# The cosine pass of a fused graph network: eight blocks pruned from the product, a moved wait, and a new order on ScalarE

## The chip, the cores and the metric

One Trainium2 chip, one core. The metric is the device time of one execution in microseconds; the kernel before takes 1676.99 us (median of 3 runs, 1675.86 to 1677.04).

## The reference, cut to what matters

Four layers on a graph of N = 3327 nodes with 64 features; `adj` is a dense 3327x3327 float32 matrix with few entries that are not zero. The first three layers are not touched. The fourth runs this twice (it = 0, 1), and only the lines from `cos` to `connectivity` are computed by the changed stage:

```python
att = softmax(Q @ edge_feat.T * scale * H, axis=1); att_scores = att.mean(axis=0)
comp_mask = softmax(0.5*structural + 0.5*att_scores) >= th_comp
x_comp = x * comp_mask[:, None];  xn = x_comp / max(norm(x_comp), 1e-8)
cos = xn @ xn.T
edge_scores = softmax(cos * H, axis=1)
edge_mask = (edge_scores >= th_edge) & comp_mask[:, None]
H_pruned = H * edge_mask
connectivity = H_pruned.sum(axis=1)            # and H_pruned.sum(axis=0)
agg = (H_pruned.T * dv_isqrt) @ transformed * de_inv
x = relu(dv_isqrt * (H_pruned @ agg) @ Theta)
```

## The kernel before, in words

The matrix is padded to 26 row blocks (NB) of 128 rows by 3328 columns, 1.7 MB each, and is streamed from HBM again in every pass. Each of the two iterations runs five passes over the 26 blocks: edge, att, cos, down, up. Rows lie as two halves of 1664 columns (HALF). Engines wait for each other by hand-written counting semaphores; each engine's program is one fixed order.

The **cosine pass** for block k, engine by engine:

- TensorE makes `cos` in four pieces of 2x416 columns in PSUM (`piece`), and for block k-2 sums the columns of the pruned rows (`columns`, which then raises `block_done`).
- VectorE (`cosine_pass`): four times `product_piece` (L1543: PSUM times the adjacency rows in the slot, into the product buffer `prod[k % 2]`, with the row maximum), then `product_max` (L1554, `negmax`), then `prune(k-1)`. Piece 0 of block k waits until the product buffer is free: for `product_free` (ScalarE's sign of block k-2) and for `share_marked` (GpSimd's marks of block k-2).
- ScalarE, the loop that calls `exps`, `sum_share` and `sign`: the exponential of block k over the product (L1247, with the row sum), then the sum of GpSimd's share of block k-1 (L1272), then `sign(k)` (L1263), which writes one mask byte for every column into the arena; the bytes are what `down` and `up` prune with later (L1730, L1759), and here `prune` too.
- GpSimd (`cut_of`, `prune_share`), for the first 24 blocks (SHARED): when the exponential of block k is done it makes the row's threshold `cut` (L637), then the marks of the last 288 columns of each half (SHARE, L647) and multiplies these columns of the slot by them (L650).
- `prune(k)` on VectorE: for k < 24 the first 1376 columns of each half (OWN), slot times (mask byte <= 0), after `sign(k)` (L1694). The last two blocks have no GpSimd share; VectorE makes their `cut` (L1681) and prunes all 3327 columns by comparing the product with `cut` (L1699).

In ScalarE's loop and in VectorE's pass the order is:

```python
for k in range(NB):                      # ScalarE
    exps(f"cos{it}", k)
    if 0 < k <= SHARED:
        sum_share(k - 1)
    sign(k)
```

The cosine pass keeps its blocks in four slots. SyncE issues the load of block k+4 into the slot of block k when `columns(k)` and `sum_share(k)` are both done (L538 and the wait behind it in `late_stream`). The last four blocks stay for the down pass; the first three loads of the down pass go into memory that the cosine pass frees at its very end, the rest into slots that are free once the down pass has used them. Behind the cosine pass stand the row sums, a softmax over nodes, and the down pass.

Below, E(k) is the start of the exponential of block k on ScalarE.

Of the kernel before, what the change touches and what calls it, by code (L numbers as in the profile page):

```python
# [24 lines left out]
ALU = mybir.AluOpType  # L25
# [8 lines left out]
NB = (N + P - 1) // P  # L34
# [77 lines left out]
def place(row):  # L112

    return 2 * (row % HB) + row // HB
# [40 lines left out]
SHARE = 288  # L155
OWN = HALF - SHARE
SHARED = NB - 2
PRUNES = NB + NB - KEPT_BLOCKS


# [47 lines left out]
def build_program(nc, adj, adj_t, x_nodes, early_weights, late_weights, rows, bq, consts, decay_consts, x_kept, out):  # L208
    ctx = ExitStack()
    with ctx:  # L210
        def sb(name, cols, dt):
            return ctx.enter_context(nc.sbuf_tensor(name, [P, cols], dt))

        def sem(name):
            return ctx.enter_context(nc.semaphore(name))
# [9 lines left out]
        prod = [pairs[:, i * NP:(i + 1) * NP] for i in range(2)]  # L225
# [63 lines left out]
        cut = sb("cut", 2, F32)  # L289
# [29 lines left out]
        def halves(t):  # L319

            return t.rearrange("p (h n) -> p h n", h=2)
# [90 lines left out]
        row_cut = sem("row_cut")  # L412
        pruned = sem("pruned")
        share_marked = sem("share_marked")
# [76 lines left out]
        def _(sp):  # L491
# [36 lines left out]
            def late_stream(name, source, first=0, last=NB):  # L528
                kind, it = name[:-1], int(name[-1])
                for k, row in enumerate(ROW_ORDER[kind]):  # L530
# [4 lines left out]
                    behind = free - 1 - BASE[f"cos{it}"]  # L535
                    if kind in ("cos", "down") and 0 <= behind < SHARED:

                        sp.wait_ge(share_summed, it * SHARED + behind + 1)  # L538
                    if name == "edge1" and home > 5 and k < 8:
# [8 lines left out]
                    if kind == "down" and home == 8 and k < 7:  # L548

                        sp.wait_ge(piece_read, (2 * it + 2) * NB * 4 + 5)  # L550
                        sp.wait_ge(pruned, it * PRUNES + NB - 1)
                        sp.wait_ge(product_free, (2 * it + 2) * NB + 1)
                    if kind == "down" and home == 5 and k < 7:

                        sp.wait_ge(pruned, it * PRUNES + NB)
                        sp.wait_ge(product_free, (2 * it + 2) * NB + 2)
# [50 lines left out]
        def _(pool):  # L607
# [22 lines left out]
            def cut_of(it, k):  # L630

                pool.wait_ge(piece_read, ((2 * it + 1) * NB + k) * 4 + 4 + 5)
                pool.memset(prod[k % 2][:, N:NP], -HUGE)
                pool.wait_ge(exp_done, (2 * it + 1) * NB + k + 1)
                one = slice(k % 2, k % 2 + 1)
                at = place(ROW_ORDER["cos"][k])
                pool.tensor_scalar(cut[:, one], rowsum[:, one], thresholds(it)[1], small["blocked"][:, at:at + 1],  # L637
                                   ALU.mult, ALU.add).then_inc(row_cut, 1)

            def prune_share(it, k):  # L640
# [3 lines left out]
                pool.wait_ge(row_cut, it * NB + k + 1)  # L644
                if it * SHARED + k:
                    pool.wait_ge(share_pruned, it * SHARED + k)
                pool.tensor_scalar(marks, product, cut[:, k % 2:k % 2 + 1], None, ALU.is_ge)\  # L647
                    .then_inc(share_marked, 1)
                pool.wait_ge(share_marked, it * SHARED + k + 1)
                pool.tensor_tensor(slot, slot, marks, ALU.mult).then_inc(share_pruned, 1)  # L650
# [8 lines left out]
            for it in range(2):  # L659
# [8 lines left out]
                pool.tensor_scalar(tiny["unused_step"][:, :], ones32[:, 0:1], 1.0, None, ALU.mult).then_inc(steps_ready, 1)  # L668
                for k in range(SHARED):
                    cut_of(it, k)  # L670
# [7 lines left out]
        def _(pe):  # L678
# [222 lines left out]
            def product(name, left, right):  # L901
# [19 lines left out]
                def columns(k):  # L921
# [4 lines left out]
                    else:  # L926
                        pe.wait_ge(pruned, it * PRUNES + k + 1)
                        if k < SHARED:
# [62 lines left out]
            for it in range(2):  # L991
# [69 lines left out]
                def turn(pair, it=it):  # L1061

                    for g, rows_ in enumerate((range(16), range(16, NB))):
                        if pair:
                            pe.wait_ge(turned_sbuf, it * NB + 2 * (pair - 1) + g + 1)
                        for q in rows_:
                            last = pe.transpose(ps[:, 4 * BANK + q * D:4 * BANK + (q + 1) * D].bitcast(BF16),  # L1067
                                                sign_pairs[:, q * HALF + pair * P:q * HALF + (pair + 1) * P],
                                                ident_b[:, :])
                        last.then_inc(turned_psum, 1)  # L1070

                pe.wait_ge(down_ready, 2 * it + 1)
                for k in range(NB):
                    if k == NB - 1:
                        pe.wait_ge(edeg_read, it + 1)
                        turn(0)
                    pe.wait_ge(pruned, it * PRUNES + NB + max(0, k - KEPT_BLOCKS + 1))
                    if k == KEPT_BLOCKS:
# [36 lines left out]
        def _(act):  # L1115
# [104 lines left out]
            for it in range(2):  # L1220
# [22 lines left out]
                def exps(name, k):  # L1243
                    bufs = products_of(name)
                    act.wait_ge(negmax_ready, PRODUCTS.index(name) * NB + k + 1)
                    b = k % len(bufs)
                    act.activation(bufs[b][:, 0:N], bufs[b][:, 0:N], ACT.Exp, bias=negmax[:, b:b + 1],  # L1247
                                   accum_out=rowsum[:, b:b + 1]).then_inc(exp_done, 1)
# [11 lines left out]
                def sign(k):  # L1260
                    act.wait_ge(row_cut, it * NB + k + 1)
                    row = ROW_ORDER["cos"][k]
                    act.activation(interleaved(sign_marks[:, row * NP:(row + 1) * NP]), halves(prod[k % 2][:, 0:NP]),  # L1263
                                   ACT.Sign, bias=cut[:, k % 2:k % 2 + 1], scale=-1.0, saturate=False)                        .then_inc(product_free, 1)
# [9 lines left out]

                for k in range(NB):
                    exps(f"cos{it}", k)
                    if 0 < k <= SHARED:
                        sum_share(k - 1)
                    sign(k)
                root(small["structural"][:, :], small["edeg"][:, :], deg_sq, it + 1, deg_rt)  # L1280
                node_exp(2 * it + 1)
                act.wait_ge(colsum_psum, 2 * it + 2)
# [55 lines left out]
        def _(dve):  # L1338
# [190 lines left out]
            def product_piece(name, k, c):  # L1529
                g, bufs = PRODUCTS.index(name), products_of(name)  # L1530
                if c == 0:
                    landed(dve, name, k)
                    if name.startswith("cos"):

                        dve.wait_ge(product_free, g * NB + k + 1)
                        if k >= 2:
                            dve.wait_ge(share_marked, g // 2 * SHARED + min(k - 1, SHARED))
                    elif k >= 3:

                        dve.wait_ge(product_free, g * NB + k - 2 + 2)  # L1540
                        dve.wait_ge(tail_weighted, g // 2 * ADDED + min(k - 2, ADDED))
                dve.wait_ge(piece_ready, (g * NB + k) * 4 + c + 1)
                dve.tensor_tensor_reduce(out=pieces3(bufs[k % len(bufs)], c),  # L1543
                                         in0=pieces_psum(piece_place(name, k, c)[0]),
                                         in1=pieces3(slot_of(name, k), c), scale=1.0, scalar=-3.0e38, op0=ALU.mult,
                                         op1=ALU.max, accum_out=max4[:, 4 * (k % 2) + c:4 * (k % 2) + c + 1])\
                    .then_inc(piece_read, 1)
# [63 lines left out]
            for it in range(2):  # L1611
# [3 lines left out]
                for c in range(0 if it else 1, 3):  # L1615
# [21 lines left out]
                                              op1=ALU.mult))  # L1637
# [4 lines left out]
                def weigh(k):  # L1642
# [8 lines left out]
                                              in1=S["imp"][:, 2 * TAIL:NB], op0=ALU.mult, op1=ALU.add))  # L1651
# [33 lines left out]
                def prune(k):  # L1685
                    slot = slot_of(f"cos{it}", k)
                    row = ROW_ORDER["cos"][k]
                    conn = S["conn"][:, place(row):place(row) + 1]
                    if k < SHARED:

                        dve.wait_ge(product_free, (2 * it + 1) * NB + k + 3)
                        own = halves(slot[:, :])[:, :, 0:OWN]
                        marks = interleaved(signs[:, row * NP:(row + 1) * NP])[:, :, 0:OWN]
                        dve.scalar_tensor_tensor(out=own, in0=marks, scalar=0.0, in1=own, op0=ALU.is_le, op1=ALU.mult,  # L1694
                                                 accum_out=conn).then_inc(pruned, 1)
                    else:

                        dve.wait_ge(row_cut, it * NB + k + 1)
                        dve.scalar_tensor_tensor(out=slot[:, 0:N], in0=prod[k % 2][:, 0:N],  # L1699
                                                 scalar=cut[:, k % 2:k % 2 + 1], in1=slot[:, 0:N], op0=ALU.is_ge,  # L1700
                                                 op1=ALU.mult, accum_out=conn).then_inc(pruned, 1)
                cosine_pass(f"cos{it}", cut_of, prune)


                dve.wait_ge(pruned, it * PRUNES + NB)
                dve.wait_ge(share_summed, (it + 1) * SHARED)
# [5 lines left out]
                def degrees():  # L1712
# [9 lines left out]
                                              op0=ALU.is_ge, op1=ALU.mult))  # L1722
# [48 lines left out]
                for k in range(2, NB):  # L1771
                    up(k)
                    if it == 1 and k == NB // 2:
# [3 lines left out]
                                                 op0=ALU.mult, op1=ALU.mult)  # L1777
# [116 lines left out]
```

## Time and profile before

| | |
|---|---|
| median of 3 runs | 1676.99 us |
| the profiled execution: time, span | 1675.23 us, 1673.4 us |
| TensorE busy | 1476.8 us, 88% of the span |
| VectorE busy | 1140.3 us, 68% |
| ScalarE busy | 729.7 us, 44% |
| GpSimd busy | 349.3 us, 21% |
| HBM, mean over the span | 345 GB/s |
| cosine pass, iteration 0 | from 664.5 us to 849.3 us of the span |
| cosine pass, iteration 1 | from 1273.5 us to 1458.6 us |

Busy shares are means over stages that have different limits. What a stage is worth is read in that stage: by the idle time in front of each instruction and what ended it.

### The profile page before, as it was taken

The numbers are of one execution on the slowest core, as the hardware profiler recorded it, in microseconds if no ns is written. First come the engines' busy times: TensorE is split into PE (matmuls) and PEld (weight loads), VectorE is DVE, ScalarE is ACT, GpSimd is POOL, SyncE is SP. The second block draws the span as 40 slices with busy tenths as digits, with TensorE's granted clock in tenths as the row PEclk, the third lists the DMA queues.
The fourth block names the chain that finished last, engine by engine and source line by source line (L and its number), as shares of the span: only waits on it lengthen the run. The fifth ranks groups of instructions, "written<-read, shape, count | busy, mean of one in ns | idle before, by whom it ended". The sixth has DMA issues, their size and how long they took to land.

```text
span 1673.4 us, 24337 instructions
## 1 busy us (share of the span) xinstructions
PE 1476.8 (88%) x10187; PEld 634.7 (38%) x10187; DVE 1140.3 (68%) x1615; ACT 729.7 (44%) x665; POOL 349.3 (21%) x305
## 2 busy tenths in 40 slices
PE   6789999999999999677888799999997887798896
PEld 2234434434344344333332344443343333332443
DVE  0000213677611998999989799206997999999897
ACT  0000101533211675999940243023776999900443
POOL 0000000000000795444400000002993444200000
PEclk9999999999999999999899999999999889999999
DMA  9979598799799997466689999999993767699995
GB/s 401 427 314 409 213 426 341 253 317 411 298 424 386 426 425 307 168 246 245 241 326 427 424 413 423 427 426 423 420 410 147 253 246 258 232 405 426 426 425 208
DMA packets 62620, 578.41 MB, mean 346 GB/s; under 512 B 6320, under 2 KB 6576, under 8 KB 23472
## 3 DMA queue, kind: packets, MB, share of 16 engines
q1 hardware_dynamic: 62512, 576.87, 85.3%
q8 instruction: 80, 1.31, 0.3%
q14 instruction: 28, 0.23, 0.0%
HBM read 575.14 MB, written 1.70 MB: 345 GB/s over the span
## 4 chain that ended last, share of the span: by engine, by line
PE 56%; DMA 18%; DVE 16%; issue 7%; ACT 2%; SPq 0%; POOL 0%; DVEq 0%; POOLq 0%; ACTq 0%
PE ps L685 54%; DMA arena<-adj_t 9%; DMA slot<-adj 5%; DVE slot L1730 4%; DVE shared L1543 4%; DVE slot L1759 2%; DMA shared<-adj_t 2%; DVE shared L1730 2%; DMA slot<-adj_t 2%; DMA arena<-adj 1%; PE ps L1067 1%; DVE shared L1759 1%; ACT shared L1294 1%; ACT shared L1247 1%; DVE slot L1699 0%
## 5 line engine op out<-in xcount | busy, mean ns | idle before, releaser
L685 PE MATMUL ps<-shared 64*128 64x416 f32 (+3 forms) x1292 | 280.0, 474 | 89.1 <-DVE max L1543 86.3
L1543 DVE CUSTOM_DVE_ANT_1 shared<-ps,slot 128x832 f32<-128x832 f32 x352 | 342.0, 1021 | 5.7 <-PE ps L685 5.1
L1247 ACT ACTIVATE shared<-shared,negmax 128x3327 f32<-128x3327 f32 x88 | 270.1, 3069 | 68.1 <-DVE negmax L1554 65.5
L685 PE MATMUL ps<-slot,cur 128*64 128x512 f32 (+1 forms) x1440 | 262.9, 515 | 17.0 <-DVE slot L1730 14.8
L622 POOL TENSOR_SCALAR cur<-shared,row_rz 128x768 f32<-128x768 f32 x32 | 70.5, 2204 | 866.7 <-DVE row_rz L1645 862.1
L685 PE MATMUL ps<-arena 64*128 64x416 f32 (+1 forms) x1072 | 208.4, 525 | 1.5 <-DVE max L1543 0.9
L1294 ACT ACTIVATE shared<-ps 128x2048 int16<-128x2048 int16 (+1 forms) x52 | 78.1, 1554 | 276.1 <-PE ps L1067 276.0
L685 PEld LDWEIGHTS ps<-shared 64*128 64x128 f32 (+2 forms) x1292 | 113.6, 162 | 222.3 <-DVE max L1543 130.8
L685 PEld LDWEIGHTS ps<-slot,cur 128*64 128x64 f32 x1440 | 96.6, 137 | 179.7 <-issue 154.5
L1263 ACT ACTIVATE arena<-shared,cut 128x3328 fp8e4<-128x3328 f32 x52 | 159.0, 3059 | 2.1 <-DVE cut L1681 1.2
L1694 DVE SCALAR_TENSOR_TENSOR slot<-arena,slot 128x2752 f32<-128x2752 int8 x48 | 145.0, 3021 | 5.4 <-ACT arena L1263 5.4
L685 PE MATMUL ps<-shared,cur 128*64 128x512 f32 (+1 forms) x672 | 125.9, 522 | 15.5 <-DVE shared L1730 7.7
L1351 DVE COPY shared<-ps 128x512 f32<-128x512 f32 x3 | 2.1, 692 | 191.6 <-PE ps L685 191.6
L685 PEld LDWEIGHTS ps<-arena 64*128 64x128 f32 (+1 forms) x1072 | 87.3, 175 | 109.6 <-issue 69.1
L1759 DVE SCALAR_TENSOR_TENSOR slot<-shared,slot 128x3328 f32<-128x3328 int8 x32 | 114.5, 3621 | 10.7 <-ACT shared L1294 8.5
L685 PE MATMUL ps<-slot,ones 128*32 128x128 f32 (+3 forms) x1456 | 106.3, 422 | 6.7 <-DVE slot L1699 6.7
L685 PE MATMUL ps<-shared,arena 128*64 128x320 bf16 (+4 forms) x798 | 105.4, 360 | 0.4 <-DMA shared<-adj 0.4
L685 PE MATMUL ps<-slot,arena 128*64 128x512 f32 x496 | 90.8, 515 | 4.1 <-DMA slot<-adj 4.1
L1189 ACT ACTIVATE shared<-ps 128x512 int16<-128x512 f32 x104 | 53.7, 517 | 88.9 <-PE ps L685 88.6
L1123 ACT ACTIVATE shared<-ps 128x640 f32<-128x640 f32 (+1 forms) x6 | 3.9, 650 | 196.9 <-PE ps L685 196.9
L1730 DVE SCALAR_TENSOR_TENSOR slot<-arena,slot 128x3328 f32<-128x3328 int8 x24 | 85.9, 3622 | 2.9 <-DMA slot<-adj 2.9
L647 POOL TENSOR_SCALAR share_marks<-shared,cut 128x576 bf16<-128x576 f32 x48 | 82.4, 1717 | 4.7
(203 smaller groups left out, 1596.6 us busy)
## 6 DMA issues: line engine op xcount, KB each, us to landing
slot<-adj SPq DMA_DIRECT2D x157, 1664.0 KB, 9.8
slot<-adj_t SPq DMA_DIRECT2D x60, 1664.0 KB, 14.1
arena<-adj_t SPq DMA_DIRECT2D x52, 832.0 KB, 6.6
shared<-adj SPq DMA_DIRECT2D x26, 1664.0 KB, 13.9
arena<-adj_t SPq DMA_DIRECT2D x25, 1664.0 KB, 22.9
shared<-adj_t SPq DMA_DIRECT2D x22, 1664.0 KB, 14.8
arena<-adj SPq DMA_DIRECT2D x15, 1664.0 KB, 14.9
slot<-adj SPq DMA_DIRECT2D x2, 1024.0 KB, 18.8
```

What stands on the lines that cost most here:

```text
L622: weighted = pool.tensor_scalar(halves(dst), product, row_rz[:, k % 3:k % 3 + 1], None, ALU.mult)
L647: pool.tensor_scalar(marks, product, cut[:, k % 2:k % 2 + 1], None, ALU.is_ge)\
L685: return pe.matmul(o, l, r, start=start, stop=stop, skip_group_check=True)
L1067: last = pe.transpose(ps[:, 4 * BANK + q * D:4 * BANK + (q + 1) * D].bitcast(BF16), sign_pairs[:, q * HALF + pair * P:q * HALF + (pair + 1 ...
L1189: act.activation(dst, bank(c, w), ACT.Relu).then_inc(relu_act, 1)
L1247: act.activation(bufs[b][:, 0:N], bufs[b][:, 0:N], ACT.Exp, bias=negmax[:, b:b + 1], accum_out=rowsum[:, b:b + 1]).then_inc(exp_done, 1)
L1263: act.activation(interleaved(sign_marks[:, row * NP:(row + 1) * NP]), halves(prod[k % 2][:, 0:NP]), ACT.Sign, bias=cut[:, k % 2:k % 2 + 1] ...
L1294: act.activation(turned[pair % 2][:, cols], ps[:, 4 * BANK:4 * BANK + HALF].bitcast(I16)[:, cols], ACT.Copy)\
L1543: dve.tensor_tensor_reduce(out=pieces3(bufs[k % len(bufs)], c), in0=pieces_psum(piece_place(name, k, c)[0]), in1=pieces3(slot_of(name, k), ...
L1694: dve.scalar_tensor_tensor(out=own, in0=marks, scalar=0.0, in1=own, op0=ALU.is_le, op1=ALU.mult, accum_out=conn).then_inc(pruned, 1)
L1730: dve.scalar_tensor_tensor(out=slot, in0=interleaved(signs[:, row * NP:(row + 1) * NP]), scalar=0.0, in1=slot, op0=ALU.is_le, op1=ALU.mult ...
L1759: dve.scalar_tensor_tensor(out=slot, in0=marks, scalar=0.0, in1=slot, op0=ALU.is_le, op1=ALU.mult).then_inc(up_pruned, 1)
```

## The change

A new constant: the first eight blocks of each cosine pass (`BY_PRODUCT`) are pruned on VectorE from the product and the row's `cut`. It does so as the last two blocks are pruned already, but over its own 2x1376 columns only. Because `prune(k)` of these blocks now reads the product buffer, piece 0 of blocks 2 to 9 waits for VectorE's own `pruned` count. The wait for GpSimd's marks (`share_marked`) moves from piece 0 to piece 3, the only one whose columns GpSimd reads. On ScalarE `sign(k)` now comes before `sum_share(k - 1)`.

```diff
+BY_PRODUCT = 8
@@ ScalarE, cosine pass
                 for k in range(NB):
                     exps(f"cos{it}", k)
+                    sign(k)
                     if 0 < k <= SHARED:
                         sum_share(k - 1)
-                    sign(k)
@@ VectorE, product_piece
                     if name.startswith("cos"):
                         dve.wait_ge(product_free, g * NB + k + 1)
-                        if k >= 2:
-                            dve.wait_ge(share_marked, g // 2 * SHARED + min(k - 1, SHARED))
+                        if 2 <= k < BY_PRODUCT + 2:
+                            dve.wait_ge(pruned, g // 2 * PRUNES + k - 1)
...
+                if c == 3 and name.startswith("cos") and k >= 2:
+                    dve.wait_ge(share_marked, g // 2 * SHARED + min(k - 1, SHARED))
@@ VectorE, prune(k)
-                    if k < SHARED:
+                    if k < BY_PRODUCT:
+                        dve.wait_ge(row_cut, it * NB + k + 1)
+                        own, scores = (halves(t)[:, :, 0:OWN] for t in (slot[:, :], prod[k % 2]))
+                        dve.scalar_tensor_tensor(out=own, in0=scores, scalar=cut[:, k % 2:k % 2 + 1], in1=own,
+                                                 op0=ALU.is_ge, op1=ALU.mult, accum_out=conn).then_inc(pruned, 1)
+                    elif k < SHARED:
```

## Rows read from the trace of the kernel before

**Rows 1.** Busy time of each engine over the cosine pass, iteration 0.
```profile
core 0: us, PE busy (x) PEld busy (x) DVE busy (x) ACT busy (x) POOL busy (x), PEclk, DMA share, GB/s
668.70:841.90 173.20, 126.57 (x1056) 57.02 (x1058) 169.60 (x275) 169.12 (x123) 81.18 (x97) 0.95 0.60 217
```
**Rows 2.** Timeline of VectorE, one block: start, duration, instruction, count [idle before].
```profile
689.27 3.02 DVE L1694 SCALAR_TENSOR_TENSOR slot<-arena,slot 128x2752 f32<-128x2752 int8 x1
692.22 0.08 DVE L1694 DVE_READ_ACCUMULATOR slot<-arena,slot 128x1 f32 x1
692.22 1.02 DVE L1543 CUSTOM_DVE_ANT_1 shared<-ps,slot 128x832 f32<-128x832 f32 x1
...
695.99 0.08 DVE L1543 DVE_READ_ACCUMULATOR2_ANT max<- 128x1 f32 x1
696.11 0.16 DVE L1554 TENSOR_REDUCE negmax<-max 128x1 f32<-128x4 f32 x1
696.19 3.02 DVE L1694 SCALAR_TENSOR_TENSOR slot<-arena,slot 128x2752 f32<-128x2752 int8 x1
```
**Rows 3.** Timeline of ScalarE, the same block.
```profile
689.35 3.07 ACT L1247 ACTIVATE shared<-shared,negmax 128x3327 f32<-128x3327 f32 x1
...
692.42 0.67 ACT L1272 ACTIVATE share_sink<-slot 128x576 bf16<-128x576 f32 x1
...
693.08 3.06 ACT L1263 ACTIVATE arena<-shared,cut 128x3328 fp8e4<-128x3328 f32 x1
696.30 3.07 ACT L1247 ACTIVATE shared<-shared,negmax 128x3327 f32<-128x3327 f32 x1 [0.16 <-DVE negmax L1554]
```
**Rows 4.** Timeline of ScalarE, blocks 0 and 1 of the pass, iteration 0.
```profile
668.67 3.07 ACT L1247 ACTIVATE shared<-shared,negmax 128x3327 f32<-128x3327 f32 x1 [7.68 <-DVE negmax L1554]
...
672.24 3.07 ACT L1263 ACTIVATE arena<-shared,cut 128x3328 fp8e4<-128x3328 f32 x1 [0.41 <-POOL cut L637]
675.21 3.05 ACT L1247 ACTIVATE shared<-shared,negmax 128x3327 f32<-128x3327 f32 x1
...
678.26 0.67 ACT L1272 ACTIVATE share_sink<-slot 128x576 bf16<-128x576 f32 x1
```
**Rows 5.** Timeline of ScalarE, blocks 0 and 1 of the pass, iteration 1.
```profile
1277.73 3.07 ACT L1247 ACTIVATE shared<-shared,negmax 128x3327 f32<-128x3327 f32 x1 [7.68 <-DVE negmax L1554]
...
1281.30 3.07 ACT L1263 ACTIVATE arena<-shared,cut 128x3328 fp8e4<-128x3328 f32 x1 [0.41 <-POOL cut L637]
1284.27 3.05 ACT L1247 ACTIVATE shared<-shared,negmax 128x3327 f32<-128x3327 f32 x1
```
**Rows 6.** Timeline of GpSimd, block 0, iteration 0.
```profile
671.94 0.27 POOL L637 TENSOR_SCALAR cut<-rowsum,blocked 128x1 f32<-128x1 f32 x1 [3.20 <-ACT shared L1247]
672.31 1.74 POOL L647 TENSOR_SCALAR share_marks<-shared,cut 128x576 bf16<-128x576 f32 x1
674.13 1.28 POOL L650 TENSOR_TENSOR slot<-slot,share_marks 128x576 f32<-128x576 f32 x1
```
**Rows 7.** Timeline of VectorE, the first pruning of the pass.
```profile
675.34 3.02 DVE L1694 SCALAR_TENSOR_TENSOR slot<-arena,slot 128x2752 f32<-128x2752 int8 x1 [2.72 <-ACT arena L1263]
```
**Rows 8.** Timelines of ScalarE and VectorE, block 25, iteration 0, then iteration 1.
```profile
841.91 3.07 ACT L1247 ACTIVATE shared<-shared,negmax 128x3327 f32<-128x3327 f32 x1
845.59 3.68 DVE L1699 SCALAR_TENSOR_TENSOR slot<-shared,cut,slot 128x3327 f32<-128x3327 f32 x1
...
1451.27 3.07 ACT L1247 ACTIVATE shared<-shared,negmax 128x3327 f32<-128x3327 f32 x1
1454.94 3.68 DVE L1699 SCALAR_TENSOR_TENSOR slot<-shared,cut,slot 128x3327 f32<-128x3327 f32 x1
```
**Rows 9.** DMA issues at the end of the pass (timeline of SyncE's queue).
```profile
841.76 7.91 SPq L564 DMA_DIRECT2D shared<-adj  x3
856.75 8.71 SPq L564 DMA_DIRECT2D slot<-adj  x4
```
**Rows 10.** Busy time behind the pass, in the down pass (columns as in rows 1).
```profile
856.00:900.00 44.00, 40.52 (x229) 15.32 (x227) 39.70 (x19) 0.00 (x0) 0.00 (x0) 1.00 0.98 408
```
**Rows 11.** The loads of the cosine pass, by line.
```profile
DMA to landing us min/median/max: 6.6/6.8/7.4
```
**Rows 12.** Busy time of a block with the clock dip (columns as in rows 1).
```profile
797.10:804.00 6.90, 6.54 (x44) 3.04 (x44) 6.87 (x12) 6.78 (x7) 3.36 (x5) 0.75 0.57 199
```

## The prediction

> **What bounds the kernel now.** I read the timeline of each engine inside the cosine pass, because shares over the whole span mix stages. Over the pass VectorE is busy 169.60 of 173.20 us and ScalarE 169.12, while TensorE and GpSimd have room [rows 1]. So two engines are nearly full, and the question is which one paces. One block of VectorE goes from prune to prune in 696.19 - 689.27 = 6.92 us with nothing idle in between [rows 2]. In the same block ScalarE runs exponential, share sum, sign, and then stands 0.16 us for VectorE's `negmax` [rows 3]. VectorE paces, ScalarE follows 0.1 to 0.2 us behind.
>
> What ScalarE would need if it paced: exponential to next 3.07 (692.42 - 689.35), share sum to next 0.66 (693.08 - 692.42) [rows 3], sign to next 2.97 (675.21 - 672.24) [rows 4]: 6.70 us, 0.22 under VectorE. The point to see is what that leaves out. After the exponential GpSimd must turn the row sum into `cut` before the sign may start. In block 0 nothing stands between the two, and the sign starts 3.57 us after the exponential (672.24 - 668.67, with 0.41 idle, released by GpSimd's cut) [rows 4], the same in iteration 1 (1281.30 - 1277.73) [rows 5]. From block 1 on the share sum of 0.66 us fills that hole, so it costs nothing.
>
> **The change, part by part.**
>
> *Order on ScalarE.* The sign moves ahead of the share sum, so the hole of block 0 opens in each of the blocks 1 to 23, and the share sum comes behind the sign as work of its own. ScalarE's block becomes 3.57 + 2.97 + 0.67 = 7.21 us [rows 3, 4]. That is above VectorE's 6.92, so ScalarE becomes the pace: +0.29 a block.
>
> *Pruning by product.* The same form of instruction over 3327 columns takes 3.68 us with two float inputs [rows 8], that is 3.68 * 2752/3327 = 3.04 for the new shape against 3.02 by bytes [rows 2]: nothing per block. What it buys is the start: `prune(0)` now needs only `cut` (672.21 [rows 6]) and not the sign, so the 2.72 us that VectorE stood there [rows 7] go. But the next exponentials on ScalarE do not move: E(1) = 675.21 follows the first sign, which does not change. VectorE gets a lead that the slower engine cannot use.
>
> *The wait for `pruned`.* It is VectorE waiting for its own last instruction. An instruction without a wait starts with the accumulator read in front of it (692.22 and 692.22), one with such a wait 0.12 later (695.99 to 696.11) [rows 2]: 0.12 us in 8 blocks an iteration. VectorE's block is then 7.04 to 7.06, still under 7.21: nothing. Bound if VectorE did pace: 16 * 0.12 = 1.9 us. Queued behind the wait are the pieces and `negmax`, for which ScalarE waits; they are early by over 2 us.
>
> *The marks wait at piece 3.* GpSimd's marks of block k-2 end long before piece 0 of block k (1.74 us after `cut` [rows 6], five us before the piece): it cost nothing and costs nothing. With pruning by product VectorE may run close behind `cut`; then piece 3 is the one to wait, with 2.8 us of the other pieces in front.
>
> *The mask-byte blocks, 8 to 23.* `prune(k)` can start when the sign ends, at E(k) + 3.57 + 2.97 = E(k) + 6.54. Prune 2.95, pieces and `negmax` of block k+2 about 4.05: done at E(k) + 13.54. ScalarE wants that `negmax` at E(k+2) = E(k) + 14.42. So 0.9 us spare: ScalarE stays the pace here too.
>
> *Loads.* `sum_share(k)` also releases the load of block k+4. It now ends at about E(k+2), 3.4 us later in the cycle; landing takes 6.8 us [rows 11], so the block is there at E(k+2) + 7.0. Piece 0 could use it at E(k+2) + 6.54, and must have it by E(k+4) - 4.1 = E(k+2) + 10.3. Late by 0.5 for VectorE, early by 3.3 for the pace: nothing. If landing took over 10 us the loads would pace.
>
> *Sum.* Iteration 0: E(1) = 675.21 stays. E(24) = 675.21 + 23 * 7.21 = 841.04. The cut of block 24 is VectorE's; I take 7.1 for that block, E(25) = 848.14, against 841.91 [rows 8]. Last pruning: before, 3.68 after E(25), since VectorE was still busy with `prune(24)`; now it is free, and exponential with accumulator 3.19 + cut 0.19 = 3.38 (cut by the same distance as before). 851.52 against 845.59: +5.93. Iteration 1: 1284.27 [rows 5] + 23 * 7.21 + 7.1 + 3.38 = 1460.58 against 1454.94 [rows 8]: +5.64. Together +11.57 us.
>
> *Does it reach the end?* The first three loads of the down pass are issued from 841.76 on within 7.91 us and the next four from 856.75 [rows 9]; the three wait for reads of the pass's last two blocks, the four for the down pass itself. Behind them the DMA engines are 98% busy at 408 GB/s [rows 10] and stay near full up to the next cosine pass (page, DMA line). A queue that is full from then on starts later by what the pass ends later; nothing absorbs it. One to one, in both iterations.
>
> So the profiled execution, 1675.23 us, becomes 1686.8; it stands 1.76 under the median of the runs, so for the median I say 1676.99 + 11.6 = **1688.6 us**. Own range of this case: the period is read to 0.03 us, 47 blocks, and E(25) to some tenths: 1686 to 1691.
>
> **A rule that speaks against the change.** The rows show GpSimd and VectorE's prune side by side only for 0.07 us: GpSimd's multiply ends at 675.41 [rows 6], the prune starts at 675.34 and takes the 3.02 of all others [rows 7]. That tells neither way what happens if they overlap. The Trainium skill (SBUF — State Buffer, Who interferes with whom) says that a VectorE instruction with two SBUF inputs and a GpSimd instruction that reads SBUF exclude each other for the whole instruction. No run here shows it yet. By my times the sum is the same with it: see the third rival.
>
> **The rivals.**
>
> 1. *The cut's round trip stays hidden; faster.* If the sign could start 3.07 after the exponential, ScalarE's block would be 6.71, VectorE would pace, and its 2.72 us at the start [rows 7] would be kept less 8 * 0.12: 1.76 an iteration, 3.5 in all, 1673.5 us. It decides where the hole between exponential and sign is under about 0.2 us. Against it: 0.41 idle in both iterations where nothing stands between [rows 4, 5]. Chance 0.06.
> 2. *Nothing at all, or partly absorbed.* If the pass's end did not gate the later loads, or if ScalarE's spare and VectorE's lead made the period 6.9 to 7.1: 1677 to 1685. Against: [rows 9, 10]. No change 0.05 (1677), partly 0.08 (1683).
> 3. *The exclusion makes `cut` late.* GpSimd's `cut(k)` is wanted at E(k) + 3.27. A prune that runs then would hold it and with it ScalarE, for up to 3.02 us. By product, `prune(k-1)` starts after the marks of k-1, ends at about E(k) + 1.2; by bytes it ends at E(k) + 2.5, 0.8 early. So it should miss. If every second of the 16 product blocks were hit by half a prune: 8 * 1.5 = 12 us more, 1701. This is what the rule quoted above from the Trainium skill would do. Chance 0.06.
> 4. *TensorE's clock.* Some blocks now run a part at the lower level (1.2 GHz): 6.54 us of TensorE work in 6.90 at a granted clock of 0.75 [rows 12], hidden. At full clock that is 6.54 * 0.75 = 4.9 us; a whole block at 1.2 GHz would be 9.8 us, above 7.21, 2.6 us a block. Five such blocks: 1702. Chance 0.03.
>
> **How the numbers follow.** Main case 0.72, 1688.6. A measurement of this kernel tells about 0.2% (3.4 us) from no change. Faster: rival 1, of which nearly all lies at that bound, 0.06. Same: 0.05. Slower, the main case, the partly absorbed one, and rivals 3 and 4: 0.89. Range: the main case with its own width, the upper part of "partly absorbed" and a little above: 1682 to 1692. Left out: rivals 1, 3, 4, no change: 0.20.
>
> **What the changed profile should show.** ScalarE: sign 3.57 after each exponential with 0.4 idle released by GpSimd's cut, 7.21 from exponential to exponential, no idle for `negmax`. VectorE: no 2.72 idle at the first prune, new idle of 0.1 to 0.3 a block at piece 0 (product blocks) or at the mask-byte prune, released by ScalarE's sign. The last L1699 ends at about 855.2 and 1470 (shifted by the first). The first loads of the down pass near 847.5. The prediction is wrong if ScalarE's period is under 7 us, or if the pass ends 6 us later and the down pass does not.

## The result and the profile after

The changed kernel takes 1685.88 us (median of 5 runs, 1685.71 to 1688.1) against 1676.99 us (5 runs, 1675.86 to 1677.72). The medians lie 8.9 us apart; the ratio is 1.0058, 95% interval 1.0045 to 1.007, that is 9.7 us slower. The forecast was 1688.6 us with a range of 1682 to 1692. The profiled execution has a span of 1684.1 us, 10.7 more than before.

First ScalarE, the timeline of one block of the changed kernel (start, duration, instruction, count, [idle before and its releaser]). L1248 is the exponential, L1264 the sign, L1273 the share sum:

```profile
682.14 3.06 ACT L1248 ACTIVATE shared<-shared,negmax 128x3327 f32<-128x3327 f32 x1
...
685.70 3.07 ACT L1264 ACTIVATE arena<-shared,cut 128x3328 fp8e4<-128x3328 f32 x1 [0.41 <-POOL cut L638]
688.67 0.67 ACT L1273 ACTIVATE share_sink<-slot 128x576 bf16<-128x576 f32 x1
...
689.34 3.05 ACT L1248 ACTIVATE shared<-shared,negmax 128x3327 f32<-128x3327 f32 x1
```

From exponential to sign it is 3.56 us, from sign to share sum 2.97, from share sum to the next exponential 0.67: 7.20 us where [rows 3] had 6.95 and a wait for `negmax` at its end. That wait is gone, and the idle time of block 0 between exponential and sign [rows 4] stands in every block. ScalarE's list of waits in iteration 0, first of the changed kernel (us in total, times, longest), says the same:

```profile
ACT arena L1264 <- POOL cut L638: 9.7, 24, 0.4
```

and of the kernel before:

```profile
ACT shared L1247 <- DVE negmax L1554: 2.2, 12, 0.5
```

VectorE and GpSimd in the changed kernel (timelines; L1697 is the prune by product, L1704 the prune by mask bytes, L1547 a piece, L648 the marks, L651 the multiply). The first prune no longer waits for the sign [rows 7], and VectorE then runs until it has used its lead:

```profile
672.27 3.38 DVE L1697 SCALAR_TENSOR_TENSOR slot<-shared,cut,slot 128x2752 f32<-128x2752 f32 x1
...
675.89 1.02 DVE L1547 CUSTOM_DVE_ANT_1 shared<-ps,slot 128x832 f32<-128x832 f32 x1 [0.23 <-DVE slot L1697]
...
679.87 3.08 DVE L1697 SCALAR_TENSOR_TENSOR slot<-shared,cut,slot 128x2752 f32<-128x2752 f32 x1
...
687.17 3.08 DVE L1697 SCALAR_TENSOR_TENSOR slot<-shared,cut,slot 128x2752 f32<-128x2752 f32 x1
...
701.92 4.19 DVE L1697 SCALAR_TENSOR_TENSOR slot<-shared,cut,slot 128x2752 f32<-128x2752 f32 x1
...
767.93 3.03 DVE L1704 SCALAR_TENSOR_TENSOR slot<-arena,slot 128x2752 f32<-128x2752 int8 x1 [0.19 <-ACT arena L1264]
```

```profile
672.04 1.74 POOL L648 TENSOR_SCALAR share_marks<-shared,cut 128x576 bf16<-128x576 f32 x1
673.87 2.93 POOL L651 TENSOR_TENSOR slot<-slot,share_marks 128x576 f32<-128x576 f32 x1
...
680.37 3.72 POOL L651 TENSOR_TENSOR slot<-slot,share_marks 128x576 f32<-128x576 f32 x1
...
701.95 1.28 POOL L651 TENSOR_TENSOR slot<-slot,share_marks 128x576 f32<-128x576 f32 x1
```

Three things are to be seen. A product block takes VectorE 687.17 - 679.87 = 7.30 us, not the 7.05 of the prediction, with 0.23 idle at piece 0 that its own prune released. GpSimd's multiply, 1.28 in [rows 6], takes 2.93 and 3.72 here, when a prune is running, and up to 4.18 in others of these blocks; and one prune in each pass is the one that gets longer, 4.19 in this one, where it and a multiply start within 0.03 us of each other and the multiply keeps its 1.28. In the mask-byte blocks VectorE stands 0.19 us for the sign: it follows ScalarE.

The end of the pass and what follows (timelines of ScalarE, VectorE and SyncE's queue of the changed kernel; then its busy times in the down pass):

```profile
847.59 3.05 ACT L1248 ACTIVATE shared<-shared,negmax 128x3327 f32<-128x3327 f32 x1
850.96 3.68 DVE L1709 SCALAR_TENSOR_TENSOR slot<-shared,cut,slot 128x3327 f32<-128x3327 f32 x1
...
846.82 8.22 SPq L565 DMA_DIRECT2D shared<-adj  x3
...
1282.92 3.07 ACT L1248 ACTIVATE shared<-shared,negmax 128x3327 f32<-128x3327 f32 x1 [7.68 <-DVE negmax L1558]
1465.48 3.69 DVE L1709 SCALAR_TENSOR_TENSOR slot<-shared,cut,slot 128x3327 f32<-128x3327 f32 x1
```

```profile
861.50:905.50 44.00, 40.52 (x229) 15.29 (x227) 40.02 (x19) 0.00 (x0) 0.00 (x0) 1.00 0.98 408
```

The down pass looks as in [rows 10], only later. From the last prune of the first cosine pass to the first exponential of the second there are 1282.92 - 850.96 = 431.96 us, before 1277.73 - 845.59 = 432.14 [rows 5, 8]. Nothing in between took the delay up.

The experiments below are read by the length of each pass: from the start of the exponential of block 0 to the start of the last full-width prune. Each kernel has also its time and its ratio to runs of the kernel before on the same chip; these runs of before have a median of 1676.97 us for the first four experiments (e1 to e4) and 1676.38 for the last three (e5 to e7).

| kernel | pass, it. 0 | pass, it. 1 | both, against before | median us | ratio (95% interval) |
|---|---|---|---|---|---|
| before | 176.92 | 177.21 | | 1676.99 | |
| changed | 182.56 | 182.56 | +11.0 | 1685.88 | 1.0058 (1.0045 to 1.007) |
| e1_old_order | 178.30 | 178.51 | +2.7 | 1679.03 | 1.0011 (1.0002 to 1.002) |
| e2_order_only | 182.60 | 182.60 | +11.1 | 1686.86 | 1.0056 (1.0043 to 1.0068) |
| e3_waits_only | 179.48 | 179.64 | +5.0 | 1681.81 | 1.0031 (1.0019 to 1.0043) |
| e4_three_blocks | 177.43 | 177.04 | +0.3 | 1675.28 | 0.999 (0.9981 to 0.9999) |
| e5_share_320 | 176.84 | 177.52 | +0.2 | 1676.94 | 0.9998 (0.999 to 1.0007) |
| e6_multiply_after_prune | 176.75 | 176.65 | -0.7 | 1673.88 | 0.9985 (0.9976 to 0.9994) |
| e7_eight_after_prune | 178.34 | 178.51 | +2.7 | 1679.29 | 1.0017 (1.0008 to 1.0026) |

### The profile page after: what moved, and what is told of

Its sections match the earlier page's. It is cut to its first block, busy times and chain, and to the rows that moved or that the text cites. A ratio compares the mean times of both kernels' runs of the same rounds, so it can differ in the third digit from the quotient of the medians.

```text
span 1684.1 us, 24327 instructions
## 1 busy us (share of the span) xinstructions
PE 1476.4 (88%) x10161; PEld 634.6 (38%) x10187; DVE 1147.6 (68%) x1615; ACT 729.4 (43%) x665; POOL 368.4 (22%) x305
## 4 chain that ended last, share of the span: by engine, by line
PE 45%; DVE 20%; DMA 18%; issue 10%; POOL 6%; ACT 2%; SPq 0%; DVEq 0%; POOLq 0%; ACTq 0%
PE ps L686 43%; DMA arena<-adj_t 7%; DMA slot<-adj 6%; DVE shared L1547 5%; DVE slot L1740 4%; DVE slot L1697 3%; POOL share_marks L648 3%; POOL slot L651 2%; DMA shared<-adj_t 2%; DVE slot L1769 2%; DVE shared L1740 2%; DMA slot<-adj_t 1%; DMA arena<-adj 1%; PE ps L1068 1%; DVE shared L1769 1%
## 5 line engine op out<-in xcount | busy, mean ns | idle before, releaser
L1547 DVE CUSTOM_DVE_ANT_1 shared<-ps,slot 128x832 f32<-128x832 f32 x352 | 342.5, 1021 | 9.4 <-DVE slot L1697 3.8
L1248 ACT ACTIVATE shared<-shared,negmax 128x3327 f32<-128x3327 f32 x88 | 269.2, 3060 | 60.6 <-DVE negmax L1558 60.6
L1264 ACT ACTIVATE arena<-shared,cut 128x3328 fp8e4<-128x3328 f32 x52 | 159.8, 3073 | 20.7 <-POOL cut L638 19.5
L1769 DVE SCALAR_TENSOR_TENSOR slot<-shared,slot 128x3328 f32<-128x3328 int8 x32 | 114.5, 3619 | 10.7 <-ACT shared L1295 8.5
L1704 DVE SCALAR_TENSOR_TENSOR slot<-arena,slot 128x2752 f32<-128x2752 int8 x32 | 96.8, 3024 | 5.0 <-ACT arena L1264 4.9
L651 POOL TENSOR_TENSOR slot<-slot,share_marks 128x576 f32<-128x576 f32 x48 | 83.4, 1737 | 4.0
```

What stands on the lines that cost most here:

```text
L1769: dve.scalar_tensor_tensor(out=slot, in0=marks, scalar=0.0, in1=slot, op0=ALU.is_le, op1=ALU.mult).then_inc(up_pruned, 1)
```

## The experiments

**The old order in the changed kernel** (e1_old_order).

```diff
                     exps(f"cos{it}", k)
-                    sign(k)
                     if 0 < k <= SHARED:
                         sum_share(k - 1)
+                    sign(k)
```

> The changed kernel with ScalarE's order of before (share sum, then sign); pruning by product in eight blocks, the wait for VectorE's own count and the moved marks wait stay. My theory (the order alone made the loss): ScalarE falls back to 6.7 us a block, VectorE paces, with 7.29 us in the 8 product blocks (as the changed trace has them) and 6.92 in the others, less the 2.7 us at the start: within 2 us of the kernel before, 1675 to 1680. Rival (pruning by product and its own wait made the loss): about 1686, as the changed kernel. Third case: GpSimd's multiply and the product prune hold each other up on the path now, over 1 us in some of the 16 blocks: 1680 to 1690.

Measured: 1.0011, +2.7 us in the two passes. Three quarters of the loss are gone by putting one ScalarE instruction of each block back. Timelines of VectorE and ScalarE of this kernel:

```profile
687.81 4.03 DVE L1697 SCALAR_TENSOR_TENSOR slot<-shared,cut,slot 128x2752 f32<-128x2752 f32 x1
...
703.36 3.08 DVE L1697 SCALAR_TENSOR_TENSOR slot<-shared,cut,slot 128x2752 f32<-128x2752 f32 x1
...
710.65 3.08 DVE L1697 SCALAR_TENSOR_TENSOR slot<-shared,cut,slot 128x2752 f32<-128x2752 f32 x1
...
703.48 3.07 ACT L1248 ACTIVATE shared<-shared,negmax 128x3327 f32<-128x3327 f32 x1 [0.50 <-DVE negmax L1558]
```

Now VectorE paces, at 7.29 us a product block, and ScalarE waits 0.50 for it. In iteration 0 eight blocks cost 8 * 0.37 = 3.0 us, the held prune of 687.81 0.95, the first prune 0.30 (3.38 as in the changed kernel), and the start gives 2.72 back: +1.5, measured +1.4. In iteration 1 the held prune takes 3.67, that is 0.59 more, which makes +1.2, measured +1.3.

**The new order in the kernel before**, nothing else (e2_order_only).

```diff
                     exps(f"cos{it}", k)
+                    sign(k)
                     if 0 < k <= SHARED:
                         sum_share(k - 1)
-                    sign(k)
```

> The kernel before with the new ScalarE order alone (sign, then share sum). My theory: 7.19 us a block on ScalarE in both passes, +5.5 an iteration, so the whole of the change's loss: 1686 to 1688, 1.006 times before; at most some tenths more than the changed kernel, since VectorE has no lead. Rival: 1677 to 1679.

Measured: 1.0056, both passes 182.60 us, within 0.04 of the changed kernel's 182.56. ScalarE's timeline:

```profile
688.60 3.05 ACT L1247 ACTIVATE shared<-shared,negmax 128x3327 f32<-128x3327 f32 x1
...
692.15 3.07 ACT L1263 ACTIVATE arena<-shared,cut 128x3328 fp8e4<-128x3328 f32 x1 [0.41 <-POOL cut L637]
695.12 0.67 ACT L1272 ACTIVATE share_sink<-slot 128x576 bf16<-128x576 f32 x1
...
695.79 3.06 ACT L1247 ACTIVATE shared<-shared,negmax 128x3327 f32<-128x3327 f32 x1
```

The order alone makes the whole loss. With it in place the rest of the change, which costs 2.7 us by itself, costs nothing: it falls on VectorE, which has room then.

**The two waits in the kernel before**, with mask bytes everywhere (e3_waits_only).

```diff
-                        if k >= 2:
-                            dve.wait_ge(share_marked, g // 2 * SHARED + min(k - 1, SHARED))
+                        if 2 <= k < 10:
+                            dve.wait_ge(pruned, g // 2 * PRUNES + k - 1)
...
+                if c == 3 and name.startswith("cos") and k >= 2:
+                    dve.wait_ge(share_marked, g // 2 * SHARED + min(k - 1, SHARED))
```

> The kernel before with the change's two waits alone: piece 0 of blocks 2 to 9 waits for VectorE's own count of the prune in front, and the marks wait stands at piece 3. VectorE paces here, so the own wait shows at full price. As the changed trace shows it (0.23 us idle and 0.14 more from accumulator read to piece, 0.37 in all): 16 * 0.37 = 5.9 us more, about 1683. As I priced it in the prediction (0.12): 1.9 us more, 1679. If it is free: 1677.

Measured: 1.0031, +5.0 us in the passes. VectorE's timeline:

```profile
683.16 3.02 DVE L1697 SCALAR_TENSOR_TENSOR slot<-arena,slot 128x2752 f32<-128x2752 int8 x1
686.10 0.08 DVE L1697 DVE_READ_ACCUMULATOR slot<-arena,slot 128x1 f32 x1
686.42 1.02 DVE L1546 CUSTOM_DVE_ANT_1 shared<-ps,slot 128x832 f32<-128x832 f32 x1 [0.23 <-DVE slot L1697]
```

A piece that waits for the prune in front of it starts 0.32 us after the accumulator read, where one that does not starts with it [rows 2]. 16 * 0.32 = 5.1 us, which is the whole +5.0, so nothing is left for the wait moved to piece 3; no piece waits for GpSimd in VectorE's list of waits. The remaining 0.05 of a product block's 0.37 is the prune itself, 3.08 against 3.02.

**Three product blocks with the old order** (e4_three_blocks).

```diff
-BY_PRODUCT = 8
+BY_PRODUCT = 3
```

> As the first of these, with three blocks by product in place of eight. Prune(0) starts 2.7 us earlier; three own waits cost 0.37 each; the first prune by mask bytes, block 3, can't start before ScalarE's sign, which at 6.70 us a block is some 0.9 us ahead of before at that block. Theory: 0.9 us won an iteration, 1675 to 1676, about 0.999 of before. If the exclusion with GpSimd bites at the start: 1677.

Measured: 0.999, but the passes are +0.5 and -0.2 us, not -0.9 each. The timelines of VectorE and GpSimd show where the lead went:

```profile
687.62 4.03 DVE L1697 SCALAR_TENSOR_TENSOR slot<-shared,cut,slot 128x2752 f32<-128x2752 f32 x1
...
699.67 1.02 DVE L1547 CUSTOM_DVE_ANT_1 shared<-ps,slot 128x832 f32<-128x832 f32 x1 [0.61 <-PE ps L686]
...
687.50 1.28 POOL L651 TENSOR_TENSOR slot<-slot,share_marks 128x576 f32<-128x576 f32 x1
```

The multiply started 0.12 us before the prune, and the prune took 0.95 longer; then TensorE was late by 0.61. Its timeline tells why, first in this kernel, then (the last line) in the kernel before:

```profile
692.98 1.76 PE L686 MATMUL ps<-shared 64*128 64x416 f32 x4 [3.35 <-DVE max L1547]
694.67 3.20 PE L686 MATMUL ps<-slot,ones 128*32 128x384 f32 x28
...
694.20 1.71 PE L685 MATMUL ps<-slot,ones 128*32 128x384 f32 x28
```

The same 28 matmuls take 3.20 us for 1.71. From 694 to 698 us the granted clock is 0.50 here, TensorE's lower level of 1.2 GHz, after it had stood 3.35 us for VectorE; in the kernel before it is 1.00 there, after 2.05 us. In iteration 1 the prune of block 2 is held as long (4.04) and TensorE is late by 0.25. The time against before is inside what differs from profile to profile outside the passes (in this one the stretch between the two is 1.3 us shorter than before), so no gain is claimed.

**The multiply held until the prune is done**, three product blocks, old order (e6_multiply_after_prune).

```diff
                 pool.wait_ge(share_marked, it * SHARED + k + 1)
+                if k < BY_PRODUCT:
+                    pool.wait_ge(pruned, it * PRUNES + k + 1)
                 pool.tensor_tensor(slot, slot, marks, ALU.mult).then_inc(share_pruned, 1)
```

> Three blocks by product with the old ScalarE order as in the fourth run, and GpSimd's multiply of these three blocks waits until VectorE has pruned them. In the fourth run the prune of block 2 took 4.03 us, since the multiply had started 0.1 us before it. Exclusion theory: that prune takes 3.08 now, no multiply is longer than 1.3 us, the pass is 0.9 us shorter in each iteration than in the fourth run (177.4 and 177.0 us from the first exponential to the last prune), the kernel about 1.8 us under it. Rival (the 4.03 came of something else, as ScalarE reading the same buffer): it stays 4.03.

Measured: 0.9985, passes 176.75 and 176.65. Timelines of VectorE and GpSimd:

```profile
687.34 3.08 DVE L1699 SCALAR_TENSOR_TENSOR slot<-shared,cut,slot 128x2752 f32<-128x2752 f32 x1
...
695.66 3.02 DVE L1706 SCALAR_TENSOR_TENSOR slot<-arena,slot 128x2752 f32<-128x2752 int8 x1 [0.95 <-ACT arena L1266]
...
690.57 1.28 POOL L653 TENSOR_TENSOR slot<-slot,share_marks 128x576 f32<-128x576 f32 x1 [3.60 <-DVE slot L1699]
```

The prune of block 2 is at 3.08, and no multiply takes over 1.30: the exclusion theory holds, its rival falls. The gain is smaller than expected (0.7 and 0.4 an iteration under e4_three_blocks, the 0.7 with TensorE's 0.61 in it), since the first mask-byte prune then waits 0.95 for ScalarE's sign: the lead runs into ScalarE. This version is the only one with both passes shorter than before. Its runs are 2.5 us under those of before, of which the passes account for 0.7; where the rest comes from is not shown.

**The same with eight product blocks** (e7_eight_after_prune). The wait above, with `BY_PRODUCT = 8`.

> The same with eight product blocks: differs from the first run (old order, eight blocks) only in the held multiply. From the first exponential to the last prune 178.3 us in the first run; 0.95 less here, 177.4, since one prune an iteration was held by a multiply. Total 1677 to 1678.

Measured: 1.0017, passes 178.34 and 178.51 us, as in e1_old_order. The expected 0.95 did not come; VectorE's timeline has it as a wait for the sign at the first mask-byte prune instead:

```profile
732.72 3.03 DVE L1706 SCALAR_TENSOR_TENSOR slot<-arena,slot 128x2752 f32<-128x2752 int8 x1 [0.94 <-ACT arena L1266]
```

ScalarE in turn had waited 2.8 us in six share sums for the multiplies that were held back. So this run, which adds a wait to ScalarE's path, can't tell what the exclusion alone costs with eight blocks.

**A larger share for GpSimd in the kernel before** (e5_share_320).

```diff
-SHARE = 288
+SHARE = 320
```

> The kernel before with GpSimd's share 320 columns a half in place of 288, nothing of the change. VectorE's prune by bytes loses 64 columns, 0.07 us. GpSimd's marks and multiply get about 0.33 us longer, so the multiply ends about 0.2 us after the point where the prune of the same block would start (it ends 0.12 before it in the kernel before). If the two exclude each other, the prune waits for the multiply (durations over 3.1 us, or idle in front), a block takes about 7.0 us and the kernel is some 5 us slower, 1680 to 1683. If they may overlap: 48 * 0.07 = 3.3 us faster, about 1674.

Measured: 0.9998, neither case. VectorE, ScalarE and GpSimd (timelines):

```profile
703.91 2.96 DVE L1694 SCALAR_TENSOR_TENSOR slot<-arena,slot 128x2688 f32<-128x2688 int8 x1
...
710.77 2.95 DVE L1694 SCALAR_TENSOR_TENSOR slot<-arena,slot 128x2688 f32<-128x2688 int8 x1
...
717.76 2.96 DVE L1694 SCALAR_TENSOR_TENSOR slot<-arena,slot 128x2688 f32<-128x2688 int8 x1
...
700.11 0.72 ACT L1272 ACTIVATE share_sink<-slot 128x640 bf16<-128x640 f32 x1
...
700.82 3.06 ACT L1263 ACTIVATE arena<-shared,cut 128x3328 fp8e4<-128x3328 f32 x1
...
702.63 1.41 POOL L650 TENSOR_TENSOR slot<-slot,share_marks 128x640 f32<-128x640 f32 x1
```

The multiply grew by 0.13, the marks by 0.16 (1.88), less than expected, so the multiply ends at 704.04 and meets the prune for 0.1 us only, and the prune stays at 2.96. At the first prune of the pass they meet for 0.36 us (multiply from 674.90 for 1.40, prune from 675.94), and that prune takes 3.17, 0.21 more. The prune is 0.07 shorter, but two blocks take 717.76 - 703.91 = 13.85, as before (6.95 + 6.92): the prune starts at 703.91, just behind the sign's end at 703.88. So there is a loop over both engines that is as long as VectorE's own work: prune(k), pieces and `negmax` of k+2, exponential, share sum and sign of k+2, prune(k+2). In two blocks VectorE's own work lost 2 * 0.07. The loop holds one of the two prunes and one share sum: it lost 0.07 and got 0.05 back, since the share sum takes 700.82 - 700.11 = 0.71 us to the sign where [rows 3] had 0.66. So relief for VectorE wins only what it takes off this loop, here next to nothing.

## Why the prediction was right, and where it was off

The forecast of 1688.6 is 2.7 us above the median and its range holds it; the narrower range that the prediction gives for its main case, 1686 to 1691, misses it by 0.1.

*The order on ScalarE* was the term that decides, and it was read from one row, the 0.41 us idle of block 0 [rows 4, 5], which the share sum hides in every other block. Forecast 7.21 us a block, measured 7.19 to 7.20; passes +5.93 and +5.64, measured +5.64 and +5.35. e2_order_only shows that it is the whole of the loss.

*"VectorE paces"* of the kernel before was only half of it. The prune of [rows 2] starts at 696.19, and the sign of [rows 3] ends at 693.08 + 3.06 = 696.14. VectorE's own work and the loop through both engines come out at the same 6.92; e5_share_320 shows the loop. For the sum it made no difference.

*The wait for `pruned`* was mis-sized: 0.12 us forecast from a reduction that waits for the piece in front of it, 0.32 measured where a piece waits for the prune. With 0.37 more in a product block VectorE takes 7.29, above ScalarE's 7.19, and not "under 7.21". It did no harm only because VectorE had its 2.7 us of lead to spend over eight blocks, which the prediction had not counted on: that part is luck. The bound "if VectorE did pace", 1.9 us, is 5.0 by e3_waits_only.

*Pruning by product* buys the start and nothing else: right. By itself it costs 2.7 us over both passes (e1_old_order), by its wait and by one held prune a pass.

*The exclusion of GpSimd and VectorE* was a rival with 0.06 and the sum "the same with it". It does occur (multiply 2.93 to 4.18, prune 4.09 and 4.19), and `cut` was never late for it: in the changed kernel the sign waits 0.40 or 0.41 us in each of the 48 blocks with a GpSimd share, the same as where no prune runs. The mechanism is present and its price is nothing, as argued, though not every step of the argument holds: `prune(k-1)` does not start "after the marks of k-1" but as soon as `cut` is there (672.27, marks until 673.78).

*Loads and TensorE's clock* cost nothing: from E(1) on every block of both passes takes 7.19 or 7.20 us, also around 690 to 697 us, where the granted clock is 0.76. The delay reached the end one to one: +11.0 in the passes, +10.7 in the span. The medians moved by 8.9 and the ratio says 9.7; what is left to the forecast's 11.6 are the period (46 blocks by 0.01 to 0.02 us) and differences between executions.

The expected signs were there (sign 3.56 after the exponential, no idle for `negmax`, 0.19 idle at the mask-byte prune, first down-pass load at 846.82 for "near 847.5"), but one: in the product blocks the idle at piece 0 came from VectorE's own prune, not from ScalarE's sign.

## What to carry to other kernels

An instruction that stands between a producer and a wait may be there to fill the wait: before it is moved, look for the one place where it is missing (here block 0) and read what the wait costs there. A lead given to one engine is worth what the other engines can follow; here ScalarE could follow by 0.2 us a block (6.7 against 6.92). A wait of an engine for its own last instruction is not free where that engine paces (0.32 us here). And where two engines are both nearly full, add up the loop that runs over both, beside the work of each.

## What the runs showed of the hardware that was not expected

- A VectorE instruction that waits for its own predecessor's count starts 0.32 us after the accumulator read instead of with it, and the passes get longer by as much (e3_waits_only: 686.10 to 686.42, 16 such waits, +5.0 us). The Trainium skill (VectorE: DVE Perf Modes, The DRAIN you can't avoid) says of a chain of tensor_copy that a semaphore after each one costs nothing extra. No run here has such a chain; the prune raises its count in the kernel before as well, and what cost time here is the wait for it. For this form the measurement decides.
- GpSimd's multiply and VectorE's prune hold each other: the one that starts clearly first keeps its length, and the other ends later by nearly what they overlap: multiply at 687.50, prune at 687.62, prune 0.95 longer (e4_three_blocks); prune at 679.87, multiply at 680.37, multiply 3.72 for 1.28 (changed kernel). Where they start within 0.04 us of each other the profile can't order them: at 701.92 and 701.95 the prune is held, at 1316.43 and 1316.47 the multiply. Here the trace agrees with the rule of the Trainium skill (SBUF — State Buffer, Who interferes with whom) quoted in the prediction. It does not for GpSimd's marks, which read one tensor: at the start of the changed pass they ran from 672.04 for 1.74 us beside the prune of 672.27, kept their length, and the prune took 3.38 for 3.08. By the rule it should have waited 1.5 us. What these 0.30 us are is not shown: they are there too with the multiply held back (3.39 in e6_multiply_after_prune), and the prune of 679.87, beside which the marks of block 1 ran for another 0.4 us, took 3.08.
- A held prune can be followed by a slower TensorE: in e4_three_blocks TensorE stood 3.35 us behind it, the granted clock then was 0.50 from 694 to 698 us, and 28 matmuls took 3.20 us for 1.71. With the prune not held (e6_multiply_after_prune) it stood 2.39 us and the clock was 1.00 in the same stretch. One such pair of runs does not show that the longer stand brought the clock down.
